# Attention scores of groups 3 to 7 on TensorE: fp16 halves of the normalised x in place of fp32 with a loaded transposed x

## The reference, cut to what matters

```python
x = x + xattn(layernorm(x), ctx, mask, Wq, bq, Wk, bk, Wv, bv, Wo, bo)   # softmax over 77 keys
h = layernorm(x)
real = h @ cos(theta + theta_noise)
imag = h @ sin(phi + phi_noise)
x = x + sqrt(real * real + imag * imag)
```

## Time and profile before

| | us |
|---|---|
| median of 3 runs | 244.77 (244.76 to 245.19) |
| the profiled execution, its own time | 245.31 |
| its span (first to last instruction) | 243.2 |
| PE busy in it | 235.8 (97%) |
| PEld busy | 136.6 (56%) |
| DVE busy | 169.6 (70%) |
| ACT busy | 145.9 (60%) |
| POOL busy | 54.4 (22%) |

### The profile page before, as it was taken

The page is one execution under the profiler, slowest core; times in us unless marked ns, Lnnn a source line. Parts: engine busy times, 40 slices in busy tenths (PEclk is TensorE's granted clock), DMA queues, the critical chain, the costliest instruction groups (busy, mean ns, idle before and its releaser), DMA issues.

```text
span 243.2 us, 3947 instructions
## 1 busy us (share of the span) xinstructions
PE 235.8 (97%) x1260; PEld 136.6 (56%) x1260; DVE 169.6 (70%) x341; ACT 145.9 (60%) x252; POOL 54.4 (22%) x154
## 2 busy tenths in 40 slices
PE   6999999999999999999999999999999999999993
PEld 2899437457544584458544854476447744444472
DVE  1676899976897876777768775877587753873443
ACT  2222787981669347943795379546873589266442
POOL 1002175410601233023302330132104310132000
PEclk9999999999999999999999999999999999999999
DMA  6999988695258724972397258734774324413622
GB/s 192 367 428 388 377 290 158 133 352 86 46 146 210 299 82 92 255 281 93 85 252 264 108 108 237 229 160 89 232 239 175 72 57 89 172 43 86 214 92 86
DMA packets 49533, 44.80 MB, mean 184 GB/s; under 512 B 42630, under 2 KB 42886, under 8 KB 46445
## 3 DMA queue, kind: packets, MB, share of 16 engines
q1 hardware_dynamic: 48565, 43.37, 57.7%
q0 software_dynamic: 288, 1.05, 2.4%
q10 hardware_dynamic: 664, 0.18, 0.3%
HBM read 25.66 MB, written 8.39 MB: 140 GB/s over the span
## 4 chain that ended last, share of the span: by engine, by line
PE 86%; DMA 7%; SPq 3%; ACT 2%; DVE 1%; issue 0%; DVEq 0%; ACTq 0%
PE re L503 9%; PE im L503 9%; PE im L504 9%; PE re L504 9%; PE re L505 9%; PE im L505 9%; PE score_bank L551 7%; DMA angle_n<-in_theta_noise 7%; PE att L481 3%; PE att L479 2%; PE re L564 2%; PE im L564 2%; PE re L566 2%; PE im L566 2%; PE re L568 2%; PE im L568 2%
## 5 line engine op out<-in xcount | busy, mean ns | idle before, releaser
L773 ACT ACTIVATE h<-x,shift,rstd 128x512 f32<-128x512 f32 x28 | 22.7, 811 | 34.6 <-POOL shift L382 34.6
L551 PEld LDWEIGHTS score_bank<-a_keys,xTb 128*128 128x128 f32 x192 | 35.9, 190 | 8.2
L503 PE MATMUL re<-w_hi,hT 128*128 128x512 f16 x100 | 37.9, 379 | 0.0
L503 PE MATMUL im<-w_hi,hT 128*128 128x512 f16 x100 | 37.9, 379 | 0.0
L505 PE MATMUL re<-w_hi,hT 128*128 128x512 f16 x100 | 37.9, 379 | 0.0
L505 PE MATMUL im<-w_hi,hT 128*128 128x512 f16 x100 | 37.9, 379 | 0.0
L504 PE MATMUL re<-w_lo,hT 128*128 128x512 f16 x100 | 37.9, 379 | 0.0
L504 PE MATMUL im<-w_lo,hT 128*128 128x512 f16 x100 | 37.9, 379 | 0.0
L1055 DVE SCALAR_TENSOR_TENSOR h_split<-h,h_split 128x512 f16<-128x512 f32 x32 | 22.1, 692 | 20.9 <-ACT h_split L777 20.2
L551 PE MATMUL score_bank<-a_keys,xTb 128*128 128x77 f32 x192 | 32.8, 252 | 0.0
L792 ACT ACTIVATE sq_re<-re 128x512 f32<-128x512 f32 x27 | 15.8, 586 | 17.2 <-PE re L505 12.1
(11 more groups left out here) (181 smaller groups left out, 425.7 us busy)
## 6 DMA issues: line engine op xcount, KB each, us to landing
xTb<-in_xT SPq DMA_DIRECT2D x8, 1024.0 KB, 5.2
xb<-in_x SPq DMA_DIRECT2D x7, 1024.0 KB, 5.5
out_rows<-wv SPq DMA_DIRECT2D x7, 1024.0 KB, 3.9
wk<-in_Wk SPq DMA_DIRECT2D x2, 512.0 KB, 5.5
wqT<-in_WqT SPq DMA_DIRECT2D x4, 256.0 KB, 7.8
wv<-in_Wv SPq DMA_DIRECT2D x1, 1024.0 KB, 13.6
wo<-in_Wo SPq DMA_DIRECT2D x1, 1024.0 KB, 16.1
xb<-in_x SPq DMA_DIRECT2D x4, 256.0 KB, 16.2
```

The lines of the kernel that those rows point to most:

```text
L503: nc.tensor.matmul(bank_[:, :], hT[j][:, 0, k, :], w_hi[part][:, k, :], start=(k == 0), stop=False)
L551: last = nc.tensor.matmul(score_bank[:, KEYS * j:KEYS * j + KEYS], xTb[:, k, P * j:P * j + P], a_keys[:, k, KEYS * batch:KEYS * batch + KEYS],
L773: nc.scalar.activation(h[j % 2][:, :], x2[b][:, j, :], ACT.Identity, bias=shift2[:, j:j + 1], scale=rstd2[:, j:j + 1]).then_inc(h_made, 1)
```

## The change

For groups 3 to 7 (`SPLIT = 3`) the scores are made of fp16 halves, as the products of `feed` are.

- In place of `xT` the kernel normalises x itself: POOL's `shift_of_x` makes rstd1 and shift1 for a group with four instructions of 128x4, ACT's `high_of_x` makes y = x * rstd1 + shift1 (128x512) and its high half for each tile, DVE's `low_of_x` the low half, and SP's `transpose_y` sends a DMA transpose for each tile.
- `a_keys` is scaled and split once into `a_split` (in step 1, with a norm that ACT, PE, DVE and POOL work out).
- `score_halves` has two matmuls for each tile and chunk: the high half of y with both halves of the keys (154 columns), the low half with the high keys (77 columns). They now stand in both parts of tile 3, one `feed` later than before. The results go to two banks, and `logits_of_halves` reads them with two pairs of DVE instructions.
- x of the later groups is loaded to `x_of[m]` (`wqT`, `xb[1]`, `xb[0]` in turn). The buffers of y are parts of `wo` and `angle_n`, so its rows carry these names.
- `stats_of_later_x` (statistics of group n+2, with their mean) now stands right behind the row maximum on DVE. The steps are no longer a hardware loop on SP, ACT and DVE.

```diff
+            def transpose_y(m, j):
+                sp.wait_ge(y_lo_made, TILES * (m - SPLIT) + j + 1)
+                if m > SPLIT:
+                    sp.wait_ge(scores_mm, m)
+                sp.sem_inc(transposes_sent, 1)
+                sp.dma_start_transpose(yT[j]..., y_split[j]...).then_inc(yT_ready[j], 16)
...
+            def step(n):                                         # SP
+                if n + 3 < GROUPS:
                     sp.wait_ge(x2_made, TILES * (n + 1))
-                    load_x(batch, blk)
+                    load_later_x(n + 3)
                 transpose_h(n, [2])
                     transpose_probs(n + 1)
                 transpose_h(n, [3])
-                    sp.wait_ge(scores_mm, n + 2)
-                    load_xT(batch, blk)
+                if n + 2 < GROUPS:
+                    for j in range(TILES):
+                        transpose_y(n + 2, j)
                 sp.wait_ge(result_made, n)
                 sp.dma_start(out..., result[:, :, :]).then_inc(stored, 16)
                     transpose_h(n + 1, [0, 1])
...
+            def shift_of_x(m):                                   # POOL
+                if not isinstance(m, int) or m > SPLIT:
+                    pool.wait_ge(y_hi_made, TILES * (m - SPLIT))
+                rstd_of_x(m)
+                nc.gpsimd.tensor_tensor(minus_mean1, zero, mv1[:, :, 0], ALU.subtract)
+                pool.wait_ge(minus_mean1_made, m - SPLIT + 1)
+                pool.wait_ge(rstd1_made, m + 1)
+                nc.gpsimd.tensor_tensor(shift1, minus_mean1, rstd1, ALU.mult).then_inc(shift1_made, 1)
...
+            def score_halves(m, batch, i):                       # PE
+                j, k = divmod(i, CH)
+                if i == 0:
+                    pe.wait_ge(a_split_ready, 1)
+                    pe.wait_ge(scores_read, m)
+                if k == 0:
+                    pe.wait_ge(yT_ready[j], 16 * (m - SPLIT + 1))
+                nc.tensor.matmul(bank_[:, at:at + KK], yT[j][:, 0, k, :], a_split[:, BATCH * k + batch, :, :],
+                                 start=(k == 0), stop=False)
+                last = nc.tensor.matmul(bank_[:, at:at + KEYS], yT[j][:, 1, k, :], a_split[:, BATCH * k + batch, 0, :],
+                                        start=False, stop=(k == CH - 1))
...
+            pe.wait_ge(a_squared, 1)                             # PE, ahead of step 1
+            nc.tensor.matmul(pT_bank[:, 0:1], ones_all[:, :], a_part[:, :], start=True, stop=True)
...
+            def high_of_x(m, j):                                 # ACT
+                i = TILES * (m - SPLIT) + j
+                act.wait_ge(shift1_made, m - SPLIT + 1)
+                if i >= 2:
+                    act.wait_ge(y_lo_made, i - 1)
+                nc.scalar.activation(y[j % 2], x_of[m][:, j, :], ACT.Identity,
+                                     bias=shift1[:, j:j + 1], scale=rstd1[:, j:j + 1]).then_inc(y_made, 1)
+                act.wait_ge(y_made, i + 1)
+                nc.scalar.activation(y_split[j][:, 0, :], y[j % 2], ACT.Copy, scale=H_SCALE).then_inc(y_hi_made, 1)
...
                 square(n, 0, 0)
                 square(n, 0, 1)
+                if more:
+                    high_of_x(n + 2, 0)
                 roots(n - 1)
+                if more:
+                    high_of_x(n + 2, 1)
                 square(n, 1, 0)
+                if more:
+                    high_of_x(n + 2, 2)
+                    high_of_x(n + 2, 3)
                 square(n, 1, 1)
```

More of the change, by code:

```diff
@@ L322, in _ @@
             transpose_h(1, [1])
[L323 to L328, removed]
+            load_later_x(SPLIT)
+            for n in range(1, GROUPS):
+                step(n)
             for j in range(TILES - 1):
@@ L599, in step @@
                 attend(n + 1, batch, 1)
[L600 to L603, removed]
+                feed(n, 2, 1)
                 attend(n + 1, batch, 2)
                 if more:
-                    feed_and_score(n, 3, 0, n + 2, 1 - batch, 2 * CH)
+                    feed_and_score(n, 3, 0, n + 2, 1 - batch, 0)
                 else:
@@ L609, in step @@
                 attend(n + 1, batch, 3)
-                feed(n, 3, 1)
+                if more:
+                    feed_and_score(n, 3, 1, n + 2, 1 - batch, 2 * CH)
+                else:
+                    feed(n, 3, 1)
             pe.wait_ge(a_ready, CH)
@@ L669, in _ @@
             feed_first(3, 1, 1)
+            pe.wait_ge(a_squared, 1)
+            nc.tensor.matmul(pT_bank[:, 0:1], ones_all[:, :], a_part[:, :], start=True, stop=True).then_inc(a_norm_mm, 1)
             pe.wait_ge(im_squared, 2)
@@ L880, in step @@
                 high_half(n + 1, 1 - b, 2)
[L882 to L886, removed]
+            for n in range(1, LAST):
+                step(n, n % BATCH)
             square(LAST - 1, 3, 1)
@@ L967, in stats_of_second_x, with stats_of_later_x, low_of_x @@
                     last.then_inc(stats1_made, 1)
+            def stats_of_later_x(m):
+                dve.wait_ge(ld_later_x[m], 16)
+                for j in range(TILES):
+                    last = nc.vector.bn_stats(stats1[:, j, :], x_of[m][:, j, :])
+                last.then_inc(stats1_made, 1)
+                if m > SPLIT:
+                    dve.wait_ge(shift1_made, m - SPLIT)
+                dve.wait_ge(stats1_made, m + 1)
+                mean_of_x(m)
+            def low_of_x(m, j):
+                dve.wait_ge(y_hi_made, TILES * (m - SPLIT) + j + 1)
+                nc.vector.scalar_tensor_tensor(out=y_split[j][:, 1, :], in0=y[j % 2], scalar=H_SCALE,
+                                               in1=y_split[j][:, 0, :], op0=ALU.mult,
+                                               op1=ALU.subtract).then_inc(y_lo_made, 1)
             def mean_of_x(m):
@@ L1209, in step @@
                 mean_of_x2(m, 3)
-            step(1, 1, 1)
-            step(2, 0, 2)
-            step(3, 1, 2)
-            step(4, 0, 3)
-            step(5, 1, 3)
-            step(6, 0, None)
+            for n in range(1, LAST):
+                step(n, n % BATCH)
             add_squares(LAST - 1, 3)
```

136 lines of the change are left out of this document (111 added, 25 removed).

## The result

The changed kernel takes 260.5 us (median of 4 runs, 260.08 to 261.04) against 244.76: ratio 1.064, interval 1.0616 to 1.0664. The prediction was 257.5, range 250 to 264, slower with 0.91. The profiled execution took 260.3, span 258.5.

A forecast was written before the change was run, and what follows sets the result against it. The loop of DVE, ACT and POOL was to bound the kernel in place of PE: 4.2 (start, step 1) + 6.8 (steps 2 to 5) + 1.7 (step 6) = 12.7 us on 245.31, so 258.0, median 257.5; range 250 to 264.

The forecast's parts named there:

- The bound moves from PE to the loop of DVE, ACT and POOL: Steps 2 to 5: work these engines hand one another, logits to next logits, outlasts PE's step, lengthening each by 1.7 us.
- Score 0.125 us, PE's step 24.4: On PE: an fp16 score takes 0.125 us instead of 0.18, so PE's step is 24.4 us (bounds 24.0 and 25.3).
- First half of the turn, 15.1: In the DVE, ACT and POOL loop: from logits to first residual takes 15.1 us, where it was 12.9.
- Second half, 11.9: In the loop: from first residual to next logits takes 11.9 us, 11.3 of DVE work plus a 0.6 wait.
- A turn of 27.0: The whole loop, logits to next logits: 27.0 us against PE's 24.4 (bounds 26.1 and 28.0).
- Start and step 1: The loop's first turn: first residual at 90.0, first feed of step 2 at 99.0, +4.2 us for both together.
- Free in the forecast: DMA of hT behind the store: a later landing first uses up PE's 2.6 us wait, so it costs nothing.
- The signs it named: New profile: PE under 95% busy, middle steps 27.0, step 1 near 29, ACT and DVE idle at named places.
- +4.2 for step 1: The sum's term for start and step 1 together: +4.2 us, taken because some waits may overlap.
- PE stays the bound: Rival: the loop's turn stays under 24.4 us, so PE's gain pays and the time is 241.0 us; chance 0.07.
- The DMAs join in: Rival: extra transposes and the store make hT and pT land at 6.3 us instead of 2.7: 264 us; chance 0.12.
- A shorter loop: Rival: cheaper POOL instructions, logits at 0.9 or no wait give turns of 26.0 or less: 249 to 253; chance 0.12.

The follow-up runs named there:

- e4: Changed kernel with every score's two matmuls issued twice, so PE gets more work: 261.0 us, ratio 1.065.
- b4: b1 with every score's two matmuls issued twice, the same edit as e4: 251.0 us, ratio 1.0236.
- e3: Changed kernel with y, its halves and transposes made for group 3 only and reused by groups 4 to 7: 250.2 us, ratio 1.0219.
- b1: Changed kernel, all operations kept but reordered: roots ahead of squares and y, finish ahead of y's low halves, store behind hT's first transposes: 243.4 us, ratio 0.992.
- f1: Changed kernel with the 1 MB store behind the transposes of hT tiles 0 and 1 instead of ahead: 260.5 us, ratio 1.0627.
- e1: Changed kernel with the roots ahead of the first y on ACT and finish ahead of y's first low half on DVE: 255.9 us, ratio 1.0438.
- e2: Changed kernel with the store behind the first transpose of y instead of behind the fourth: 263.9 us, ratio 1.0763.
- b3: b1 with the store back ahead of the transposes of hT tiles 0 and 1, as in the changed kernel: 251.2 us, ratio 1.0246.

## Why the prediction was right

*The bound moves from PE to the loop of DVE, ACT and POOL.* Shown: e4 and b4 add the same work to PE, for 0.5 and 7.7 us; e3 takes y out of the loop, and PE is without a gap in steps 2 to 5. The clock is no rival: e4 ran at 1.00 over its span and has the same turns.

*Score 0.125 us, PE's step 24.4.* Measured 0.100 and 24.1, the lower bound: the fp16 loads don't show in these rows. Timeline of PE in the changed kernel, a pair and the product behind it:

```profile
119.59 0.23 PE L627 MATMUL score_bank<-a_split,angle_n 128*128 128x154 f16 x1
119.66 0.20 PE L629 MATMUL score_bank<-a_split,angle_n 128*128 128x77 f16 x1
119.69 0.38 PE L643 MATMUL re<-w_lo,hT 128*128 128x512 f16 x1
```

0.07 and 0.03 us, the columns alone. It had no effect on the time, as the prediction said. An estimate from the figure of the Trainium skill in "TensorE: Matmul & The Clock Gate", section Back-to-back issue gap (about 81 ns per matmul at 128 columns in a sustained stream), makes it 0.16; these rows don't agree with it, for pairs that stand between long matmuls.

*First half of the turn, 15.1.* Measured 14.6. The one step mis-sized is POOL's: of its two new 128x4 instructions one took 0.56 and the other 0.20, and the first of all 0.34. Logits, maximum, statistics, y, table load and roots came as counted (`finish` at 11.8, counted 12.3). The one wait that it put on ACT here, for POOL's shift, is not in the rows of the turns: ACT's own queue ends only 0.1 us sooner. By these rows a shorter POOL would have gained at most 0.1 us a turn in this order.

*Second half, 11.9.* Measured 12.8, and this is the term that was wrong. The work was 11.1 (counted 11.3); the waits were 0.41 + 1.29 = 1.70 us, counted 0.6. The chain behind the second wait is read from the rows: tile 2's mean at 152.82 stands behind a sum of squares, POOL's four instructions follow, the first of them at 0.55 in place of 0.19, then the high half. In b1, where the mean stands ahead of the sum, the second half is 11.8 in the turn shown; b1 moves other instructions of that half too, so what this one move is worth stays open.

*A turn of 27.0.* Measured 27.39: four turns give 1.6 of the 2.3 us by which the profiled execution (260.3) exceeds the 258.0 forecast.

*Start and step 1.* Residual 0 was forecast at 90.0 and came at 89.35; the logits of step 2 at 90.0 + 11.9 = 101.9, measured 102.17. The first feed came at 101.66 in place of the forecast's 99.0, since `hT`, issued at 96.09, landed after 5.6 us rather than 2.8. Timeline of SP in the changed kernel:

```profile
94.06 0.57 SPq L345 DMA_DIRECT2D out_rows<-wv  x1
96.09 4.01 SPq L309 DMA_TRANSPOSE hT<-h_split  x2
```

That looks like 2.7 us lost, but f1 takes the gap away and gains nothing: the next step, 26.12, gives half of it back at once, and the last one ends by the loop. "Free in the forecast" was right for the changed kernel.

*The signs it named.* PE busy 91% (under 95% forecast), idle ahead of `attend` and the first feed, and DVE idle before the first low half of y and before `finish`: all there. Step 1 was 31.7 us and not near 29, as `hT` landed late, and ACT stood idle before the first y in step 1 only.

*The 2.3 us that are missing.* Counted in the loop's frame: logits of step 2 late by 0.3 against the forecast, four turns by 1.6, from the last of them (211.73) to the first feed of step 7 (233.34) 21.6 in place of 21.5. Together 2.0. The rest is the sum's own rounding: it took +4.2 for step 1, where its working gave 4.5 (and the first feed of step 2 stood at 94.3 before the change, not at 94.5).

*The rivals.* "PE stays the bound" is false for this order, and its condition was sized too kindly: the roots' order alone gave 0.5 us a turn (e1), while b1 as a whole took 3.3 off the turn and ended at 243.4, not at 241.0. The Trainium skill, in "Perfetto Trace Analysis", section Identifying the Most-Contended Engine, ranks engines by occupancy but judges TensorE by its FLOPs and the busy share of its weight loads, not by its matmuls. The loads were busy for 56%, so by that share DVE with 70% came first, and DVE is where the added work did its harm; yet PE, with no idle time in its step, did pace the kernel before. Neither share gives the length of the loop. "The DMAs join in" didn't happen here (f1), but its mechanism is real: e2 and b3 show it at +3.4 and +7.9, both with a part that is the half clock behind PE's wait. "A shorter loop" had its POOL part right by half and its waits wrong.

## What to carry to other kernels

Work that is moved off the busiest engine has to be priced on the loop that it lands in, waits included, not on the busy share of the engines there: DVE was busy for 70%, and 14.5 us more on it, with 27.9 more on ACT, made the kernel 15.7 us slower in this order. Before an order is judged, count the loop once from one fixed instruction to itself, then ask which link stands ahead of another without need; here the same operations in another order gave 243.4 us in place of 260.5. The place of a store beside transposes on one queue was free in the long loop and cost 8 us in the short one, a third of it by the estimate through the clock, so it is to be looked at again each time the loop gets shorter.

## What the runs showed that had not been expected

**POOL beside DVE.** A 128x1 instruction took 0.19 us at 149.77, just ahead of a DVE low half (150.09), and 0.55 when it started inside one: at 153.07 against DVE's row below, and the same at 146.98 against the low half of 146.82. The 0.56 of `minus_mean` at 135.73 has a low half beside it too (135.54, 0.69), the 0.20 of `shift` at 136.37 none. The row that the prediction took its 0.55 from has a neighbour too: at 132.25 in the kernel before, inside a sum of squares on DVE (132.08, 0.66), and ending 0.06 us behind it. So that 0.55 is a price of the neighbour, not of the shape. Not every DVE instruction does it: beside residuals and statistics the simple 128x1 instructions keep their 0.19. Timeline of DVE in the changed kernel:

```profile
152.91 0.66 DVE L1194 SCALAR_TENSOR_TENSOR h_split<-h,h_split 128x512 f16<-128x512 f32 x1
```

POOL's instruction ends as the low half does (153.62 against 153.57). That one holds up the other is what the rows suggest, since the end follows the neighbour's in each of them; no run moved one of the two alone.

**The clock after a pause.** PE had a gap of 3.56 us ahead of `attend`'s tile 2 in step 1, and when it went on the granted clock was half until 93.3. Windows of the changed kernel, the pause and the stretches behind it:

```profile
86.97:90.15 3.18, 0.01 (x2) 0.01 (x1) 3.18 (x4) 3.12 (x6) 0.00 (x0) 0.96 0.00 0
90.15:93.55 3.40, 3.40 (x14) 1.63 (x15) 3.33 (x7) 1.98 (x4) 1.22 (x4) 0.54 0.81 154
93.55:97.00 3.45, 3.45 (x28) 1.94 (x27) 2.96 (x6) 2.71 (x4) 1.17 (x5) 1.00 0.96 297
```

The same place in e4, the stretch behind the pause:

```profile
90.79:94.20 3.41, 2.94 (x25) 1.61 (x25) 3.34 (x7) 1.99 (x4) 1.22 (x4) 1.00 1.08 120
```

14 matmuls in 3.4 us against 28 in the next 3.45: the lower of its two levels, 1.2 GHz. In e2 the same followed gaps of 3.7, 4.4 and 3.6 us, in e1 one of 3.2, and in b3 PE worked 5.3 us at half clock after a gap of 4.08. The gaps of 2.5 us and less in the changed kernel have none behind them. But the length of the gap alone doesn't decide: e4 has one of 3.66 at the same place (90.79), and behind it the clock is 1.00, with 25 matmuls in 3.4 us. As e4 has the same turns, the half clock isn't in the 27.4; where it does come, it costs half of the stretch, 1.6 us in the changed kernel's step 1.

**Transposes beside a store.** Three issues of `hT` behind the 1 MB store took 6.57 us in b3; two behind the transposes of y took 3.93 in b1. The prediction had the 6.3 us of its slowest row as the bound; in the changed kernel the slowest of `hT` landed after 7.7. Answer on the tile `hT` there:

```profile
DMA to landing us min/median/max: 3.0/3.1/7.7
```
